# GpSimd waits for its scatters, and at every third indirect store for all stores before it

## The chip, the cores and the metric

One core of a Trainium2 chip runs the kernel. Its engines are TensorE (PE; PEld is its weight load), VectorE (DVE), ScalarE (ACT), GpSimd (POOL) and SyncE (SP), and its DMA engines are fed by queues. The metric is the time on the device in microseconds, the median of several runs.

## The reference

The input x has 2 batches of 2048 rows with 256 columns. A first block normalises x, makes q, k and v by a two-layer perceptron with GELU each, takes causal scores without a softmax, multiplies them with v, normalises the result and adds it to x. A second block normalises again and applies to every row one of eight 256 by 256 matrices, chosen by the row's position alone:

```python
x = x + attn(layernorm(x), W1q, b1q, W2q, b2q, ..., ln_w, ln_b)
# attn: q, k, v = gelu(x@W1+b1)@W2+b2; scores = (q@k.T)/scale * tril; out = layernorm(scores@v)*ln_w+ln_b
# ffn: idx = argmax(pe @ sign(tile_sigs).T); out[b, s] = x[b, s] @ W[idx[s]].T + b[idx[s]]
x = x + ffn(layernorm(x), tile_sigs, W, b)
```

## The kernel before

**Stages.** The attention runs in 8 steps `s` of 512 rows (4 chunks of 128), four for each batch; `LAST` is 7. Front work of step s+1 (transposes, perceptrons, scores) is woven by hand with back work of step s (state, output, normalisation). Every engine has one instruction stream, in the order in which the code issues it, and waits on semaphores.

**Sorting.** A finished chunk of rows, with its scale, shift and row number, lies in `xres`. GpSimd writes its 128 rows with an indirect DMA into `sorted_rows` in DRAM, at places sorted by matrix (`rows_sorted`, line 1674, the scatter at line 1679; 30 scatters in all, semaphores `row_out[s % 3]`). `rstd_out` and `rstd_x1` are small GpSimd steps that give the scales which the rows need before they can be scattered.

**Slots.** The sorted rows are read back as 37 slots of 128 rows (`SLOTS`), n = 0 to 36, all rows of a slot with one matrix. SP loads them (`load_slot`, line 454). It loads slots from n = 17 (`FIRST`) once the scatters of steps up to 6 have landed, and slots from n = 21 (`EARLY`) once all 30 have. Slot 0 is worked alone, then come 18 pairs: pair m holds slots 2m+1 and 2m+2. For a pair ACT normalises both slots (line 982), PE transposes them (line 761), ACT and DVE split the result in two parts (lines 999 and 1429), PE multiplies with the matrix (line 491), and DVE adds the product to the rows (`pair_out`, line 1437), which raises `y_done`. From pair 8 on PE's order is transposes of pair m+2, then products of pair m. So the products of pair 8 stand behind the transposes of pair 10, whose slots are 21 and 22.

**Outs.** GpSimd stores slot n to the output with an indirect DMA (`slots`, line 1741, the store at line 1744), in the order of n; rows that are padding are dropped by the bounds check. The store of slot n is called out n here. Outs 0 to 3 (`REUSED` is 4) raise `sent[0]`, outs 4 to 36 raise `sent[1]`, by 16 each.

**Order on GpSimd in the last part.** Scatters of step 5, outs 0 to 2, `rstd_out(6)`, outs 3 to 6, `rstd_x1(6)`, four scatters of step 6, outs 7 to 12, `rstd_out(7)` of two chunks, outs 13 and 14, `rstd_x1(7)`, the last two scatters, outs 15 and 16, `rstd_out(7)` of the other two chunks, outs 17 and 18, `rstd_x1(7)`, outs 19 to 36.

**The end.** The last two chunks of rows are not sorted. They are multiplied with all eight matrices (`dense_products`, 8 groups of products) and DVE adds what is theirs (`dense_out`, line 1451); SP stores them (line 479). The program ends when these two stores and all outs have landed (lines 481 to 483).

Of the kernel before, what the change touches and what calls it, by code (L numbers as in the profile page):

```python
# [40 lines left out]
LAST = STEPS - 1  # L41
# [23 lines left out]
XR = 3  # L65
# [7 lines left out]
def mk_seq_kernel(nc, x, w1, w2, bias_cols, rows3, sigs2, ffn_w, ffn_b, pe, out):  # L73
# [5 lines left out]
    with ExitStack() as ctx:  # L79
# [6 lines left out]
        def sem(name):  # L86
            return ctx.enter_context(nc.semaphore(name))
# [137 lines left out]
        row_out = [sem(f"row_out{i}") for i in range(XR)]  # L225
# [70 lines left out]
        REUSED = SLOTS - ALL_ROWS  # L296
        in_hT = sb("slot_rows", [P, T_ROWS, ROW])

        def row_buf(n):
            i = n % ALL_ROWS  # L300
            if i < H_ROWS:
                return in_h32[:, i * ROW:i * ROW + ROW]
            return in_hT[:, i - H_ROWS]
# [71 lines left out]
        sent = [sem(f"sent{i}") for i in range(2)]  # L375
# [29 lines left out]
        def sent_before(s):  # L405

            return [16 * (CH * len(range(i, s, XR)) - (DENSE if s > LAST and i == LAST % XR else 0))
                    for i in range(XR)]
# [1198 lines left out]
        def _(pool):  # L1607
# [41 lines left out]
            def rstd_out(s, cs=range(CH)):  # L1649
                part, these = s + 1, slice(cs[0], cs[-1] + 1)  # L1650
                if s < LAST:
                    pool.wait_ge(o_sq, CH * s + CH)
                    nc.gpsimd.tensor_scalar(ve2[:, :], sq2[:, :], 1.0 / C, EPS, ALU.mult, ALU.add).then_inc(var2, 1)
                else:
                    part = s + 1 + cs[0] // 2
                    pool.wait_ge(o_aggr, cs[-1] + 1)
                    nc.gpsimd.tensor_tensor(ve2[:, these], mv2[:, these, 1], eps[:, these], ALU.add).then_inc(var2, 1)
                pool.wait_ge(var2, part)
                nc.gpsimd.tensor_tensor(rs2[:, these], ve2[:, these], half[:, these], ALU.pow).then_inc(rstd2, 1)

            def rstd_x1(s, cs=range(CH)):
                part, these = s + 1 + (s == LAST) * (cs[0] // 2), slice(cs[0], cs[-1] + 1)
                if s < LAST:
                    pool.wait_ge(aggr3, part)
                    nc.gpsimd.tensor_scalar(nm3[:, :], mv3[:, :, 0], -1.0, None, ALU.mult)
                    nc.gpsimd.tensor_tensor(ve3[:, :], mv3[:, :, 1], eps[:, :], ALU.add).then_inc(var3, 1)
                pool.wait_ge(var3, part)
                nc.gpsimd.tensor_tensor(xres[s % XR][:, these, RSTD], ve3[:, these], half[:, these], ALU.pow
                                        ).then_inc(rstd3, 1)
                pool.wait_ge(rstd3, part)  # L1670
                nc.gpsimd.tensor_tensor(xres[s % XR][:, these, SHIFT], nm3[:, these], xres[s % XR][:, these, RSTD],
                                        ALU.mult).then_inc(shift3, 1)

            def rows_sorted(s, cs):

                pool.wait_ge(shift3, s + 1 + (s == LAST) * (cs[0] // 2))
                for c in cs:
                    at = slot_i[:, s // PER, CH * (s % PER) + c:CH * (s % PER) + c + 1]
                    pool.indirect_dma_start(out=sorted_rows, out_offset=bass.IndirectOffsetOnAxis(ap=at, axis=0),  # L1679
                                            in_=xres[s % XR][:, c, :], in_offset=None).then_inc(row_out[s % XR], 16)  # L1680
# [60 lines left out]
            def slots(ns):  # L1741
                for n in ns:
                    pool.wait_ge(y_done, n + 1 if n < AMID else AMID + (n - AMID) // 2 + 1)
                    pool.indirect_dma_start(out=out_rows,  # L1744
                                            out_offset=bass.IndirectOffsetOnAxis(
                                                ap=row_buf(n)[:, PLACE:PLACE + 1].bitcast(I32), axis=0),
                                            in_=row_buf(n)[:, 0:C], in_offset=None,
                                            bounds_check=NB * T - 1, oob_is_err=False).then_inc(sent[n >= REUSED], 16)
# [21 lines left out]
            s = LAST - 1  # L1770
            residual(LAST)
            rstd_x1(s - 1)
            rows_sorted(s - 1, range(CH))
            slots((0, 1, 2))
            rstd_out(s)
            slots((3, 4, 5, 6))
            rstd_x1(s)
            rows_sorted(s, range(CH))

            slots((7, 8, 9, 10, 11, 12))  # L1780
            rstd_out(LAST, (0, 1))
            slots((13, 14))
# [60 lines left out]
```

## Time and profile before

| | us |
|---|---|
| three runs | 315.4, 316.1, 316.92 (median 316.1) |
| the profiled execution | 315.08 |
| its span | 313.3 |
| busy: PE, DVE, ACT, POOL | 289.5, 235.7, 188.7, 176.6 |
| 37 outs on POOL (line 1744), busy | 21.7 + 15.5 |
| 30 scatters on POOL (line 1679), busy | 31.3 |

The span runs from the first instruction to the last; 1.8 us of the execution lie around it. POOL is busy for 56% of the span and PE for 92%, but these are means over the whole. The last 70 us, in which the outs run, are what matters here. The busy time of a scatter or an out on POOL is the writing of its descriptors; its data move after that.

### The profile page before, as it was taken

To read this page: it belongs to the slowest core of one execution; us is meant where nothing else is said; L and a number is where in the kernel's file an instruction comes from. 1 tells how busy PE (TensorE), PEld (TensorE's weight loads), DVE (VectorE), ACT (ScalarE), POOL (GpSimd) and SP (SyncE) were. 2 spreads that over 40 slices of the span, in tenths; PEclk is the share of its full clock that TensorE was granted. 3 is DMA by queue.
4 is the path that set the end of the run, shared out by engine and by line. 5 is a ranking of instruction groups with operands and counts; after the bars stand their busy time and mean duration, and the time that the engine had idled before them with its cause. 6 is when DMAs were issued, how large, how long until landed. Compare 5 with 4: busy or idle time off the path is not lost.

```text
span 313.3 us, 5485 instructions
## 1 busy us (share of the span) xinstructions
PE 289.5 (92%) x1806; PEld 256.9 (82%) x1806; DVE 235.7 (75%) x539; ACT 188.7 (60%) x380; POOL 176.6 (56%) x238
## 2 busy tenths in 40 slices
PE   8999999998999999999999999999998976594994
PEld 6788898986898988889788988899988965583983
DVE  5868788899879879968986896798568667272556
ACT  2646777666756876676778667678664353372400
POOL 6881633351584659475646626584565757276551
PEclk9979999999999999999999999999999999699899
DMA  7909960020011110311221000250142331832011
GB/s 221 231 0 330 354 216 1 0 69 33 6 68 67 42 64 2 94 43 39 63 73 64 9 0 20 85 167 20 70 132 78 114 131 69 256 133 80 32 42 34
DMA packets 24209, 27.83 MB, mean 89 GB/s; under 512 B 4659, under 2 KB 22068, under 8 KB 24118
## 3 DMA queue, kind: packets, MB, share of 16 engines
q1 hardware_dynamic: 15910, 13.68, 14.8%
q0 software_dynamic: 3296, 8.64, 8.0%
q10 hardware_dynamic: 4976, 5.16, 4.9%
q8 instruction: 15, 0.25, 0.3%
q14 instruction: 12, 0.10, 0.1%
HBM read 13.95 MB, written 14.44 MB: 91 GB/s over the span
## 4 chain that ended last, share of the span: by engine, by line
PE 73%; DVE 11%; issue 5%; ACT 4%; another core or an unknown queue 2%; POOL 2%; DMA 1%; DVEq 0%; ACTq 0%; POOLq 0%; SPq 0%
PE ring L491 41%; PE o_ps L491 9%; PE s_ps L491 6%; PE w_ps L491 2%; ACT xn L982 2%; DVE xres L1451 2%; PE ring L500 2%; PE ring L519 2%; PE sc_ps L604 2%; PE ring L761 1%; POOL out_dram L1744 1%; PE sc_ps L602 1%; DVE xres L1219 1%; DVE xnT L1147 1%
## 5 line engine op out<-in xcount | busy, mean ns | idle before, releaser
L491 PE MATMUL ring<-xnT,w_sp 128*128 128x512 f32 x288 | 74.4, 403 | 3.0 <-DVE hT L1152 1.1
L491 PEld LDWEIGHTS ring<-xnT,w_sp 128*128 128x128 f32 x288 | 52.7, 191 | 15.2 <-issue 3.3
L882 ACT ACTIVATE ring<-ring,b_cols 128x512 f32<-128x512 f32 x48 | 31.7, 660 | 28.4 <-PE ring L491 27.0
L491 PE MATMUL ring<-hT,w_sp 128*128 128x512 f32 x192 | 46.8, 398 | 0.0
L1152 DVE TENSOR_TENSOR hT<-ring,hT 128x512 fp32r<-128x512 f32 x48 | 32.5, 681 | 14.6 <-ACT hT L885 13.0
L491 PEld LDWEIGHTS ring<-hT,w_sp 128*128 128x128 f32 x192 | 35.8, 190 | 8.3 <-DVE hT L1152 0.2
L1679 POOL DMA_INDIRECT sorted_rows<-xres,slot_i x30 | 31.3, 1044 | 8.5 <-issue 6.5
L1645 POOL TENSOR_TENSOR vtok<-v,vtok 128x512 fp32r<-128x512 f32 x14 | 18.0, 1287 | 26.5 <-ACT vtok L902 26.5
L1744 POOL DMA_INDIRECT out_dram<-slot_rows x22 | 21.7, 987 | 18.4 <-DVE slot_rows L1437 13.1
L885 ACT CAST hT<-ring 128x512 fp32r<-128x512 f32 x48 | 28.2, 587 | 1.5
L1219 DVE SCALAR_TENSOR_TENSOR xres<-cen,rs,xres 128x256 f32<-128x256 f32 x32 | 23.7, 754 | 3.2 <-issue 3.2
L491 PE MATMUL s_ps<-vtok,ktok 128*128 128x256 f32 x168 | 24.9, 284 | 0.0
L491 PEld LDWEIGHTS ring<-w_sp,hT 128*128 128x128 f32 x192 | 23.4, 188 | 0.6
L491 PE MATMUL ring<-w_sp,hT 128*128 128x256 f32 x192 | 23.9, 280 | 0.0
L1624 POOL TENSOR_SCALAR nm<-mv 128x4 f32<-128x4 f32 x7 | 1.6, 229 | 39.2 <-DVE mv L1141 39.2
L491 PE MATMUL o_ps<-state,q_eye 128*128 128x256 f32 x116 | 23.3, 293 | 0.0
L491 PEld LDWEIGHTS s_ps<-vtok,ktok 128*128 128x128 f32 x168 | 22.0, 191 | 0.0
L1638 POOL TENSOR_TENSOR xres<-xt,row_stage 128x1024 f32<-128x1024 f32 x8 | 22.0, 2751 | 0.0
L1744 POOL DMA_INDIRECT out_dram<-h x15 | 15.5, 1030 | 10.6 <-DVE h L1437 7.0
L491 PE MATMUL w_ps<-wf,xb 128*128 (+1 forms) x126 | 19.8, 307 | 1.3 <-DVE xb L1429 1.3
L491 PEld LDWEIGHTS w_ps<-wf,xb 128*128 128x128 f32 x126 | 17.9, 201 | 2.7 <-issue 1.8
L1191 DVE TENSOR_TENSOR state<-s_ps,state 128x512 fp32r<-128x512 f32 x27 | 18.3, 679 | 2.1 <-ACT state L918 1.8
(245 smaller groups left out, 680.8 us busy)
## 6 DMA issues: line engine op xcount, KB each, us to landing
sorted_rows<-blank ACTq DMA_DIRECT2D x1, 5032.0 KB, 20.8
xt<-x SPq DMA_DIRECT2D x7, 512.0 KB, 3.5
slot_rows<-sorted_rows SPq DMA_DIRECT2D x22, 136.0 KB
w_stage<-tile_w SPq DMA_DIRECT2D x8, 256.0 KB, 2.7
h<-sorted_rows SPq DMA_DIRECT2D x15, 136.0 KB
xt<-x SPq DMA_DIRECT2D x2, 256.0 KB, 3.0
hT<-position_table POOLq DMA_DIRECT2D x1, 512.0 KB, 9.2
sorted_rows<-xres,slot_i POOLq DMA_INDIRECT x30
```

What stands on the lines that cost most here:

```text
L491: last = te.matmul(o, lhs[k][a], rhs[k][c], start=start and k == 0 and i == 0, stop=stop and k == n - 1 and i == 2, skip_group_check=check)
L500: te.matmul(ring[2][:, :], warm_r[:, 0:P], warm_r[:, :], start=True, stop=True)
L519: last = te.transpose(ring[k][:, cols(c)], xn[:, c, cols(k)], ident[:, :])
L882: nc.scalar.activation(full, ring[(2 + m) % 3][:, :], ACT.Gelu, bias=b1c[:, m // 2, m % 2:m % 2 + 1]).then_inc(gelu, 1)
L885: nc.scalar.copy(hT[:, m, 0, :], full).then_inc(h_hi, 1)
L1152: nc.vector.tensor_tensor(hT[:, m, 1, :], ring[(2 + m) % 3][:, :], hT[:, m, 0, :].bitcast(F32), ALU.subtract).then_inc(h_lo_dve, 1)
L1191: nc.vector.tensor_tensor(state[:, 1, :], s_ps[:, :], state[:, 0, :].bitcast(F32), ALU.subtract).then_inc(s_lo, 1)
L1219: nc.vector.scalar_tensor_tensor(out=xres[s % XR][:, c, 0:C], in0=cen[:, c, :], scalar=rs2[:, c:c + 1], in1=xres[s % XR][:, c, 0:C], op0=A ...
L1638: nc.gpsimd.tensor_tensor(xres[s % XR][:, :, 0:C], xt[s % 2][:, :, :], lnb_row[:, :].unsqueeze(1).broadcast_to([P, CH, C]), ALU.add).then_ ...
L1645: nc.gpsimd.tensor_tensor(vtok[:, 1, 2 * j:2 * j + 2, :], v32[:, 2 * j:2 * j + 2, :], vtok[:, 0, 2 * j:2 * j + 2, :].bitcast(F32), ALU.sub ...
L1679: pool.indirect_dma_start(out=sorted_rows, out_offset=bass.IndirectOffsetOnAxis(ap=at, axis=0), in_=xres[s % XR][:, c, :], in_offset=None) ...
L1744: pool.indirect_dma_start(out=out_rows, out_offset=bass.IndirectOffsetOnAxis(ap=row_buf(n)[:, PLACE:PLACE + 1].bitcast(I32), axis=0), in_= ...
```

## The change

Three waits are added, all on GpSimd. Ahead of out n, for n above 4 and divisible by 3 (n = 6, 9, 12, ..., 36: eleven of them), it waits until `sent[1]` shows that outs 4 to n-1 have all landed. After `rstd_out(6)`, ahead of out 3, it waits until the scatters of step 5 have landed. After the four scatters of step 6, ahead of out 7, it waits until these have landed.

```diff
             def slots(ns):
                 for n in ns:
                     pool.wait_ge(y_done, n + 1 if n < AMID else AMID + (n - AMID) // 2 + 1)
+                    if n > REUSED and n % 3 == 0:
+                        pool.wait_ge(sent[1], 16 * (n - REUSED))
                     pool.indirect_dma_start(out=out_rows,
...
             slots((0, 1, 2))
             rstd_out(s)
+            pool.wait_ge(row_out[(s - 1) % XR], sent_before(s)[(s - 1) % XR])
             slots((3, 4, 5, 6))
             rstd_x1(s)
             rows_sorted(s, range(CH))
+            pool.wait_ge(row_out[s % XR], sent_before(LAST)[s % XR])
 
             slots((7, 8, 9, 10, 11, 12))
```

## Rows read from the trace of the kernel before

**Rows 1.** The page, part 4: the chain that ended last, shares by engine.
```profile
PE 73%; DVE 11%; issue 5%; ACT 4%; another core or an unknown queue 2%; POOL 2%; DMA 1%; DVEq 0%; ACTq 0%; POOLq 0%; SPq 0%
```
**Rows 2.** The same chain in order of time: start us, length us, what.
```profile
248.27 1.76 another core or an unknown queue
...
254.64 0.98 POOL out_dram L1744
...
263.74 2.43 DMA sorted_rows<-xres,slot_i
266.23 2.14 DMA slot_rows<-sorted_rows
...
282.66 4.64 another core or an unknown queue
```
**Rows 3.** Timeline of POOL, 229 to 249: start, length, instruction, [idle before <-releaser].
```profile
229.85 1.07 POOL L1744 DMA_INDIRECT out_dram<-h  x1 [0.20 <-issue]
...
245.32 0.96 POOL L1679 DMA_INDIRECT sorted_rows<-xres,slot_i  x1 [0.30 <-issue]
246.59 1.43 POOL L1744 DMA_INDIRECT out_dram<-h  x1 [0.31 <-issue]
248.32 1.00 POOL L1744 DMA_INDIRECT out_dram<-h  x1 [0.30 <-issue]
```
**Rows 4.** Timeline of POOL, 254 to 262.
```profile
254.64 0.98 POOL L1744 DMA_INDIRECT out_dram<-slot_rows  x1 [2.74 <-DVE slot_rows L1437]
255.93 0.98 POOL L1744 DMA_INDIRECT out_dram<-slot_rows  x1 [0.30 <-issue]
...
258.30 1.04 POOL L1744 DMA_INDIRECT out_dram<-slot_rows  x1 [0.36 <-issue]
259.64 0.98 POOL L1744 DMA_INDIRECT out_dram<-slot_rows  x1 [0.30 <-issue]
261.11 0.72 POOL L1668 TENSOR_TENSOR xres<-ve,half 128x2 f32<-128x2 f32 x1 [0.48 <-issue]
```
**Rows 5.** Timeline of POOL, 274 to 306.
```profile
274.75 1.04 POOL L1744 DMA_INDIRECT out_dram<-slot_rows  x1 [6.43 <-DVE slot_rows L1437]
276.10 0.99 POOL L1744 DMA_INDIRECT out_dram<-slot_rows  x1 [0.30 <-issue]
...
278.65 1.04 POOL L1744 DMA_INDIRECT out_dram<-slot_rows  x1 [0.54 <-DVE slot_rows L1437]
...
305.81 0.97 POOL L1744 DMA_INDIRECT out_dram<-h  x1 [0.30 <-issue]
```
**Rows 6.** Timeline of DVE, 253 to 301.
```profile
253.15 0.69 DVE L1437 TENSOR_TENSOR slot_rows<-w_ps,slot_rows 128x512 f32<-128x512 f32 x1
...
258.69 0.87 DVE L1219 SCALAR_TENSOR_TENSOR xres<-cen,rs,xres 128x256 f32<-128x256 f32 x2
...
260.86 0.16 DVE L1242 TENSOR_SCALAR ve<-mv 128x2 f32<-128x2 f32 x1
...
300.49 0.69 DVE L1437 TENSOR_TENSOR h<-s_ps,h 128x512 f32<-128x512 f32 x1 [3.10 <-remote]
```
**Rows 7.** Timeline of ACT, 268 to 288.
```profile
268.39 1.09 ACT L982 ACTIVATE xn<-slot_rows 128x255 f32<-128x255 f32 x2 [4.12 <-DMA slot_rows<-sorted_rows]
...
287.33 0.58 ACT L999 CAST xb<-sc_ps 128x512 fp32r<-128x512 f32 x1 [4.67 <-remote]
```
**Rows 8.** DMA busy tenths in 40 slices of 0.075 us: from 258.2, then from 305.8.
```profile
DMA  0000000000000000000000496993000000000000
...
DMA  0000110000000000000001159999510000000000
```
**Rows 9.** Timeline of SP's queue, then the landing time of its two output stores.
```profile
306.70 4.84 SPq L479 DMA_DIRECT2D out_dram<-xres  x2
...
DMA to landing us min/median/max: 1.7/1.7/1.7
```
**Rows 10.** The instructions that write `out_dram`: duration ns min/median/max, first and last start.
```profile
L1744 POOL DMA_INDIRECT out_dram<-slot_rows x22: 972/976/1042, 254.6 to 298.1; - x22
```

## The prediction

> **What bounds the kernel now.** I read the chain that ended last first. By shares it is PE for 73% of the span and POOL for 2% [rows 1], so a reader could stop there and call waits on POOL free. The same chain in order of time says more: up to about 248 us it is PE's own stream, and after that it goes through every engine in turn. It passes an out on POOL at 254.64, the last scatter at 263.74 (landed 2.43 us after its start), the load of a slot that needed that scatter (2.14 us), and only then ACT [rows 2]. ACT had been idle for 4.12 us when it got that slot at 268.39 [rows 7]. So POOL's order between 245 and 264 us decides when the last 16 slots can start. I then read POOL's timeline over the last 75 us, because all added waits stand there, and at last DVE's, ACT's and the DMA view to see how long a store takes to land.
>
> Two further things are seen. The chain has pieces that belong to no instruction, 1.76 us at 248.27 and 4.64 us at 282.66 [rows 2]; ACT's and DVE's timelines show them as waits on PE's semaphores that nobody is named for, 4.67 us before ACT at 287.33 and 3.10 us before DVE at 300.49 [rows 6, 7]. And at the very end DVE's dense work and SP's store of it are last: SP's second store ends its issue at 311.54 (306.70 + 4.84) and starts some 0.34 us before, it lands 1.7 us after, at 312.9, and the span ends 0.4 us later [rows 9]. The last out starts at 305.81 [rows 5], so POOL's stream has about 5 us of slack at the end.
>
> **The price of one wait.** Outs that follow each other start 1.28 us apart: 255.93 less 254.64 [rows 4], a busy time of 0.976 us [rows 10] and 0.30 us between. A wait for the out just before it takes the place of that distance by the landing time plus the restart. *Landing:* for the out that starts at 258.30 the DMA engines are busy until slice 28, which is 258.2 + 28 x 0.075 = 260.3, 2.0 us after its start; for the last out (305.81) POOL's few packets are seen in slices 21 to 23, up to 307.6, 1.8 us after [rows 8]. These are ends of data, without the semaphore, so they bound it from below. The scatter with its semaphore took 2.43 us [rows 2], which I take as the upper end without contention. I take 2.3 us for a full slot and 2.1 us for the late, mostly empty ones. *Restart:* no wait of POOL for an out exists in this trace. The nearest rows are outs that waited for DVE: line 1437 on DVE ended at 253.84 (253.15 + 0.69) [rows 6] and the out started at 254.64 [rows 4], 0.80 us later. A tensor instruction after a short wait restarts faster, so 0.3 us (the plain distance between two outs) is the lower end and 0.8 us my value. So an out that waits starts 3.1 us after the one before it and not 1.28 us, a price of 1.82 us (late ones 2.9 us, a price of 1.6 us); the ends are 2.1 and 3.3 us.
>
> The Trainium skill, page DMA: Bandwidth & Descriptors, section Anatomy of one DMA, gives about 2.0 us plus bytes over 436 GB/s for a DMA from GpSimd, 2.3 us for 128 KB. No row here shows its split into parts; with it for all outs the end would come some 0.8 us later than below. The same page, Rules for kernel authors, says to issue early and wait late so that the fixed time is overlapped, which speaks against the change.
>
> **Waits that cost nothing.** The wait ahead of out 3 is for scatters of step 5, which POOL started between 217 and 222 us; with 2.43 us each they are down by 225, and out 3 starts at 229.85 [rows 3]. The wait of out 6 for out 5 delays out 6 by at most 1.82 us, from 235.1 to 237.0. What is behind it, the small steps of `rstd_x1(6)`, waits for DVE until 239.2 anyway; if DVE were 1 us earlier this cover would still hold. The wait of out 15 is for out 14, 5 us and two scatters earlier: nothing.
>
> **Waits on the path to the last scatter.** Here I follow the start times.
> 1. The last scatter of step 6 starts at 245.32 [rows 3]; landed at 247.75 (2.43), restart 0.8: out 7 starts at 248.55 and not at 246.59. Out 8: 249.83.
> 2. Out 9 waits for out 8: 252.93. Out 10: 254.21. Out 11: 255.49, and not 254.64. Its own wait for DVE (2.74 us long) [rows 4] hid the first 3.5 of 4.4 us.
> 3. Out 12 waits for out 11: 258.59, and not 255.93 [rows 4]. This is the dear one, for behind it in POOL's order stands `rstd_out` of the last step, whose result DVE needs at once (line 1219 at 258.69) [rows 6].
> 4. Out 13 follows out 12 by the 2.37 us of before (255.93 to 258.30, with the two small steps between), so 260.96; out 14 at 262.30, over at 263.28. DVE starts line 1219 at about 260.65 and is through with line 1242 2.33 us later (258.69 to 261.02) [rows 6], at 263.0, so out 14 is what ends last. The step at line 1668 starts at 263.30 and not 261.11 [rows 4]: the last two scatters come 2.2 us late.
> 5. SP's load of slot 21 waits for them, ACT gets it at 268.39 + 2.2 = 270.6, and PE's transposes of pair 10 and the products of pair 8 behind them move by the same 2.2 us. No other engine has work to fill that gap: it was already idle there.
>
> **The run of outs at the end.** Out 17 waits for pair 8: 274.75 + 2.2 = 276.94 [rows 5]. Out 18 waits for out 17: 280.04. Out 19 is 2.55 us behind out 18, as before (276.10 to 278.65), 282.59; out 20 at 283.9. From there six outs wait (21, 24, ... 36). I take 3.0 us for each, the mean of full and late ones, and 2 x 1.28 for the two between: out 21 at 286.9, and out 36 five rounds of 5.56 us later at 314.7. DVE does not hold them any more: before, the outs of pair 16 waited for line 1437 at 300.49 [rows 6], and out 33 would now start at 309. Out 36 lands 2.1 us after its start, 316.8, and with the 0.4 us of before the span ends at 317.2.
>
> The dense end moves with step 5 only: 313.3 + 2.2 = 315.5 if all else stays. So POOL takes over as the bound, with 1.7 us over the dense end. The span grows by 317.2 - 313.3 = 3.9 us. The profiled execution was 315.08 us, 1.0 us under the median of the three runs, so I add the difference to both alike: 319.0 for an execution like the profiled one, and 320.0 us against the median of 316.1.
>
> **The rivals.**
> *A, dense end last.* If landing and restart together are near their lower end (2.5 us and less), POOL is done before the dense end. Then only the shift of the last scatters counts, 2.2 us or, with cheaper waits, down to 1.0 us: 317.1 to 318.3, say 318.0. For it: both terms are bounds from other instructions. Against: 0.80 us and 2.43 us are direct rows.
>
> *B, the other side: PE's late semaphores go away.* The waits on PE that nobody is named for lie where POOL has issued four or more indirect DMAs without a pause: from 241.4 to 251.9, from 278.65 to 288.6 and from 291.8 to 299.1, and none lies before 217 us, where POOL issues at most two in a row. If the run of DMAs is what holds PE's semaphores up, a pause after every third ends it. The 4.64 us at 282.66 are on the chain [rows 2], and of the 3.10 us at 300.49 [rows 6] some 0.8 us, since PE's dense products bound DVE after that. With the scatters' shift cut to 0.8 us (waits at 2.4 us) the dense end would come at 313.3 + 0.8 - 3.1 - 0.8 = 310.2 (I count 3.1 of the 4.64 us, as the work behind it catches its own pace). It decides only if POOL's outs end before that, and this needs each wait to cost under about 2.4 us from start to start: then 316.8 - 9 x 0.7 = 310.5. This gives 310.5 + 0.4 or so, 3 us faster: 313.2 us. If the stalls go but a wait costs 3.1 us, nothing is won, since POOL is last by then: the stalls are no longer on the path. For B: the places agree. Against: no row links them, and the price of a wait would have to be far below the rows.
>
> *C, the waits do not bite.* If landing is mostly done when the wait is reached, nothing changes: 316.1. Against: the out waited for is always the one just before, 1.28 us earlier, and its data are moving later than that [rows 8].
>
> *D, landing stretched.* Slot loads run at 249 to 254 and 268 to 277 us beside outs 8, 17 and 18. If a landing there takes 3.5 us, and the late ones 2.43 us, the end is 2 to 3 us later: 322.5.
>
> **How the numbers follow.** Forecast 320.0 with chance 0.70, A 0.11, B 0.06, C 0.04, D 0.09. A measurement of this kernel tells 0.5% (1.6 us) from no change. The forecast's own width: each of nine waits may be off by 0.2 us, so 318.2 to 321.8. The range takes in A and most of D: 317.4 to 322.6. Slower by over 0.5% (above 317.7): forecast, D and most of A, 0.87. Same: C, the rest of A, 0.07. Faster: B, 0.06.
>
> **What would show it.** In the profile after, out 9, 12, 18, 21 and each third one start about 3 us after the one before, the others 1.28 us. The step at line 1668 is near 263.3, ACT's first slot of the last 16 near 270.6, the last out near 314.7, and the chain ends in outs on POOL and not in DVE's line 1451. If the waits without a name at 282 and 300 are gone and the dense work ends near 310, half of B is right although the time is slower. Wrong would be: a distance of 2.4 us or less, or out 12 not ahead of DVE's line 1219.

## The result: 3.5% slower, three times the forecast loss

| | before | changed |
|---|---|---|
| median of 4 runs, us | 316.2 | 327.5 |
| lowest and highest, us | 315.4, 316.9 | 326.5, 328.4 |
| profiled execution, us (its span) | 315.1 (313.3) | 326.9 (325.2) |

The ratio is 1.035, with a 95% interval of 1.032 to 1.039. The forecast was 320.0 us with a range to 322.6: the sign was right, and the time lies outside the range.

The chain that ended last, in order of time (start, length, what), now runs through outs on GpSimd. This is its last part:

```profile
294.40 0.70 DVE slot_rows L1437
295.14 0.52 issue
296.24 0.90 issue
297.15 0.98 POOL out_dram L1746
298.43 2.14 DMA out_dram<-slot_rows
...
314.13 0.98 POOL out_dram L1746
315.41 2.07 DMA out_dram<-h
317.60 0.51 issue
318.10 1.20 POOLq L79
```

Each round is the landing of an out, two pieces of issue, and one out beside the next. That is the forecast picture, and the answer to [rows 2]. The first line is misleading. It names DVE because DVE's line 1437 ended at 295.1, just before out 24 started, but that was the work of pair 15. DVE had finished out 24's own pair, pair 11, at 285.1. What out 24 waited for was out 23, started at 292.61 (3.26 us earlier, as in the other rounds). So the path runs on through GpSimd's outs, back to outs 17 and 18. The last line is not in the forecast: a piece of GpSimd's queue at line 79, after which the span still goes on to 325.2.

The timeline of POOL shows the waits (start, length, instruction, [idle before <-who ended it]):

```profile
245.58 0.96 POOL L1679 DMA_INDIRECT sorted_rows<-xres,slot_i  x1 [0.31 <-issue]
249.99 1.00 POOL L1746 DMA_INDIRECT out_dram<-h  x1 [3.46 <-DMA sorted_rows<-xres,slot_i]
...
257.32 0.99 POOL L1746 DMA_INDIRECT out_dram<-slot_rows  x1 [0.30 <-issue]
260.60 0.98 POOL L1746 DMA_INDIRECT out_dram<-slot_rows  x1 [2.29 <-DMA out_dram<-slot_rows]
...
265.40 0.75 POOL L1668 TENSOR_TENSOR xres<-ve,half 128x2 f32<-128x2 f32 x1
266.23 0.20 POOL L1671 TENSOR_TENSOR xres<-nm,xres 128x2 f32<-128x2 f32 x1
266.72 1.04 POOL L1679 DMA_INDIRECT sorted_rows<-xres,slot_i  x1 [0.29 <-POOL xres L1671]
268.06 0.96 POOL L1679 DMA_INDIRECT sorted_rows<-xres,slot_i  x1 [0.30 <-issue]
...
315.41 0.97 POOL L1746 DMA_INDIRECT out_dram<-h  x1 [0.30 <-issue]
318.33 0.97 POOL L1746 DMA_INDIRECT out_dram<-h  x1 [1.94 <-DMA out_dram<-h]
```

Out 12 starts 3.28 us behind out 11, the last out 2.92 us behind the one before it. The last scatter starts at 268.06, where it was 263.74 [rows 2], and the last out at 318.33, where it was 305.81 [rows 5]. ACT and DVE answer [rows 6, 7]:

```profile
272.70 1.15 ACT L982 ACTIVATE xn<-slot_rows 128x255 f32<-128x255 f32 x2 [10.48 <-DMA slot_rows<-sorted_rows]
...
287.59 0.59 ACT L999 CAST xb<-sc_ps 128x512 fp32r<-128x512 f32 x1 [0.75 <-PE sc_ps L761]
...
308.63 1.07 DVE L1451 SCALAR_TENSOR_TENSOR xres<-o_ps,w_stage,xres 128x256 f32<-128x256 f32 x2 [0.33 <-PE o_ps L491]
```

ACT's line 999 waits 0.75 us and no longer 4.67, and DVE's dense work ends at 309.70. Before, it ended at 311.2:

```profile
310.11 1.07 DVE L1451 SCALAR_TENSOR_TENSOR xres<-o_ps,w_stage,xres 128x256 f32<-128x256 f32 x2
```

So the late waits are gone, and the dense end came earlier although its start moved 4.3 us later.

What comes after the last out is seen with the instructions of line 79, the end of the program (count, duration ns, first and last start). Before:

```profile
L79 POOLq DRAIN  x1: 9007/9007/9007, 303.4 to 303.4; - x1
```

Changed:

```profile
L79 POOLq DRAIN  x1: 6830/6830/6830, 318.1 to 318.1; - x1
L79 SPq COMPARE_BRANCH  x1: 38/38/38, 320.5 to 320.5; - x1
...
L79 SPq EVENT_SEMAPHORE  x1: 17/17/17, 325.1 to 325.1; - x1
```

GpSimd's drain ended at 312.4 before (303.4 + 9.0) and at 324.9 now. Both are 6.6 us after the start of the last out, and 5.6 us after its 0.97 us of issue. SP had all landings by 320.5 and then had to wait for it. So GpSimd's stream did not have 5 us of slack at the end: it had about 0.5 us (312.4 against the dense landing at 312.9). The last out moved by 12.5 us (305.81 to 318.33) and the span grew by 11.9. The sentence ahead of the prediction that the program ends when all stores have landed leaves this drain out.

The granted clock was lower, 0.954 over the span against 0.977. It isn't what cost the time: PE's wait for the late scatters lies in there, and the way from ACT's first late slot to out 17 took 6.42 us (272.70 to 279.12) where it had taken 6.36 (268.39 to 274.75).

### The profile page after: what moved, and what is told of

Same layout as the page of the kernel before. It is cut to its first block, busy times and chain, and to the rows that moved or that the text cites. A ratio compares the mean times of both kernels' runs of the same rounds, so it can differ in the third digit from the quotient of the medians.

```text
span 325.2 us, 5498 instructions
## 1 busy us (share of the span) xinstructions
PE 287.7 (88%) x1806; PEld 254.8 (78%) x1806; DVE 235.9 (73%) x539; ACT 188.9 (58%) x380; POOL 176.5 (54%) x238
## 4 chain that ended last, share of the span: by engine, by line
PE 68%; DVE 10%; issue 7%; DMA 5%; ACT 4%; POOL 4%; POOLq 1%; SPq 0%; ACTq 0%; DVEq 0%
PE ring L491 39%; PE o_ps L491 9%; PE s_ps L491 5%; POOL out_dram L1746 3%; DMA out_dram<-slot_rows 3%; ACT xn L982 2%; PE ring L500 2%; PE w_ps L491 2%; PE ring L519 1%; PE sc_ps L604 1%; PE ring L761 1%; PE sc_ps L602 1%; DVE xres L1219 1%; DVE xnT L1147 1%; PE sc_ps L761 1%
## 5 line engine op out<-in xcount | busy, mean ns | idle before, releaser
L1746 POOL DMA_INDIRECT out_dram<-h x15 | 14.8, 990 | 20.1 <-DMA out_dram<-h 7.9
L491 PE MATMUL w_ps<-wf,xb 128*128 (+1 forms) x126 | 18.8, 295 | 1.0 <-DVE xb L1429 1.0
L491 PEld LDWEIGHTS o_ps<-state,q_eye 128*128 128x128 f32 x116 | 18.5, 189 | 1.3 <-issue 0.3
```

What stands on the lines that cost most here:

```text
L491: last = te.matmul(o, lhs[k][a], rhs[k][c], start=start and k == 0 and i == 0, stop=stop and k == n - 1 and i == 2, skip_group_check=check)
L1746: pool.indirect_dma_start(out=out_rows, out_offset=bass.IndirectOffsetOnAxis(ap=row_buf(n)[:, PLACE:PLACE + 1].bitcast(I32), axis=0), in_= ...
```

## The experiments

Each ratio is against the kernel before on the same chip, with its 95% interval.

### Only the waits for scatters

```diff
+            pool.wait_ge(row_out[(s - 1) % XR], sent_before(s)[(s - 1) % XR])
             slots((3, 4, 5, 6))
...
             rows_sorted(s, range(CH))
+            pool.wait_ge(row_out[s % XR], sent_before(LAST)[s % XR])
```

> Only the two waits for scatters, none at the outs. Theory (a wait costs only where it moves the last two scatters or the last out): out 7 starts near 249.7 us of the span, the outs behind it 1.28 us apart catch up with DVE's work by out 11, the last scatters move by 0.4 us at most, and the time is that of the kernel before within 0.6 us (316.2). Rival (the wait for the scatters alone is a large part of the loss, since it came out 1.4 us dearer than forecast): 318 or more.

Ratio 1.0012 (0.9986 to 1.0038). Out 7 started at 249.29, 4.26 us after the last scatter of its group (245.03), and the last scatter at 264.18. Outs 8 to 11 ran 1.3 to 1.5 us apart, and out 11 was at 254.65, where it had stood before. The wait is dearer than forecast, but it is covered, since out 11 had waited for DVE before. Alone it costs nothing that can be measured.

### Only the waits at outs 6 to 18

```diff
+                    if n in (6, 9, 12, 15, 18):
+                        pool.wait_ge(sent[1], 16 * (n - REUSED))
```

> Only the waits at outs 6, 9, 12, 15 and 18; outs 19 to 36 run without a pause. Theory: the last two scatters move by about 2.3 us (outs 9 and 12), and since outs 19 and on run without a pause, ACT's unexplained wait on PE near 285 us of the span (4.7 us in the kernel before) is there again; the time is 318.0 to 319.0. Rival (that wait has nothing to do with pauses in GpSimd's DMAs and merely did not happen after the shift): the wait stays away and the time is 314 to 316.5.

Ratio 1.015 (1.011 to 1.019), 320.3 us. The last scatter came 24.4 us after the first scatter of the group before it started (240.70 to 265.07). Before, that was 22.4 us (241.36 to 263.74): a shift of 2.0 us, near the expected 2.3. But the late wait did not only come back, it was twice as long. ACT's timeline:

```profile
287.08 1.09 ACT L982 ACTIVATE xn<-h 128x255 f32<-128x255 f32 x2
297.99 0.58 ACT L999 CAST xnT<-ring 128x512 fp32r<-128x512 f32 x1 [9.81 <-remote]
```

PE stood idle for 9.29 us there, and in the 6 us from 300 on it had a granted clock of 0.59. Both fit a loss above the expected 2 to 3 us; how much each cost wasn't measured. This execution (321.7) was also the slowest of four, so the 9.81 us need not be typical. The rival, that the wait had merely not happened, fell.

### Only the waits from out 21 on

```diff
+                    if n >= 21 and n % 3 == 0:
+                        pool.wait_ge(sent[1], 16 * (n - REUSED))
```

> Only the waits at outs 21, 24, ... 36. The scatters stay where they were. Theory (the program ends about 5.6 us after GpSimd's last DMA instruction, by its drain): out 36 starts near 311.6 us, the drain ends near 318.2 us, the time is 321 (5 us slower), and ACT's unexplained wait at 283 to 287 us is gone. Rival (the end is set by the landing of the last out, as the forecast had it): out 36 lands at 313.9, the span ends at 314.3 and the time is 317.2.

Ratio 1.017 (1.014 to 1.019), 320.7 us. The last out started at 312.24, and the instructions of line 79 say:

```profile
L79 POOLq DRAIN  x1: 6830/6830/6830, 312.0 to 312.0; - x1
L79 SPq COMPARE_BRANCH  x1: 38/38/38, 314.4 to 314.4; - x1
...
L79 SPq EVENT_SEMAPHORE  x1: 17/17/17, 319.0 to 319.0; - x1
```

All had landed by 314.4, and the span ended 4.7 us later with the drain. ACT and DVE had no wait without a name after 260 us, and DVE's dense work ended at 305.4 and not at 311.2. So the same pauses brought the dense end 5.8 us forward and GpSimd's end 6.4 us back.

### Only the last three outs wait

```diff
+                    if n in (34, 35, 36):
+                        pool.wait_ge(sent[1], 16 * (n - REUSED))
```

> Only waits at outs 34, 35 and 36, each for all outs before it; nothing else depends on these outs. Theory (drain): out 36 starts 3 x 1.7 us later, near 310.9 us of the span, the drain ends 6.6 us after that start at 317.5, and the time is 320.5 (4.3 us slower). Rival (landing): out 36 lands at 313.0, just at the dense end, and the time is 316.2 to 316.8. ACT's unexplained wait at 283 to 287 us stays in both, as the outs before 34 run without a pause.

Ratio 1.010 (1.007 to 1.013), 318.2 us. Nothing depends on these outs but the end of the program. The last out started at 309.37, the drain ended 6.6 us later at 316.0, and SP had all landings at 312.7. The landing rival is refuted. The loss is smaller than expected, mainly because out 33 started at 299.46 in this run and not at 302.0.

### The changed kernel without its wait at out 12

```diff
-                    if n > REUSED and n % 3 == 0:
+                    if n > REUSED and n % 3 == 0 and n != 12:
```

> The changed kernel without its wait at out 12, all other waits as they are. Theory (out 12 stands ahead of the steps that the last two scatters need, and everything behind is in one chain on GpSimd): out 12 starts 1.28 us behind out 11 and not 3.28, the last scatter and the last out move 2.0 us earlier, and the time is 2.0 us under that of the changed kernel (8.5 to 9.5 us over the kernel before). Rival (DVE's or PE's work sets the last scatters by then): under 0.5 us is won.

Ratio 1.032 (1.027 to 1.036), where the changed kernel had 1.035; the two intervals overlap, so the medians alone don't settle it. The traces do: the last scatter started at 266.32 and not 268.06, the last out at 316.43 and not 318.33, and the span was 323.3 and not 325.2. One wait, 1.9 us.

### Two waits only, at outs 22 and 26

```diff
+                    if n in (22, 26):
+                        pool.wait_ge(sent[1], 16 * (n - REUSED))
```

> Only two waits, at outs 22 and 26, for all outs before them. Theory (PE's unexplained late semaphores come after four or more indirect DMAs in a row; GpSimd's drain sets the end 6.6 us after the last out starts): outs 19 to 21, 22 to 25 are short runs, so ACT's wait near 285 us is gone; the last out starts near 304.3 us and the drain ends at 310.9, 2 us before the end of the kernel before; a late wait may come back after 295 us, in the run of outs 26 to 36, and cost a part. Time 0.3 to 2.2 us under the kernel before. Rival (each wait costs its 1.9 us at the end, as in the run with waits from out 21 on): 1 to 3 us over it.

Ratio 0.9954 (0.9936 to 0.9972): faster than before. The last out started at 304.17 (304.3 expected). From 291.37 on eleven outs ran without a pause, and the late waits came back, in the dense work. DVE's timeline:

```profile
307.02 1.07 DVE L1451 SCALAR_TENSOR_TENSOR xres<-ring,w_stage,xres 128x256 f32<-128x256 f32 x2 [3.17 <-remote]
```

### A pause by other work, without a wait for a landing

```diff
+                    if n >= 21 and n % 3 == 0:
+                        if n > 21:
+                            pool.wait_ge(idle_s, n // 3 - 7)
+                        nc.gpsimd.tensor_tensor(idle_t[:, :, :], row_stage[:, 0:2, :], row_stage[:, 0:2, :],
+                                                ALU.add).then_inc(idle_s, 1)
```

> No wait for a landing; in place of the waits at outs 21, 24, ... 36 GpSimd adds two 512-column tiles (about 1.3 us, result unused, a side product that leaves the output alone). Theory a (any pause in the run of DMA instructions on GpSimd ends PE's late semaphores): the waits without a name between 280 and 301 us are gone, DVE's dense work ends near 305.5, the last out starts near 308.3 and the drain ends at 314.9: 1 to 2.5 us slower than the kernel before. Theory b (it is the landing that must be waited for): the wait of 4 to 5 us near 285 us stays, DVE's dense work ends at 311 or later.

Ratio 0.9984 (0.9964 to 1.0004). POOL's timeline of one round:

```profile
285.59 1.07 POOL L1749 TENSOR_TENSOR idle_t<-row_stage 128x512 f32<-128x512 f32 x1
286.82 0.99 POOL L1751 DMA_INDIRECT out_dram<-slot_rows  x1 [0.17 <-POOL idle_t L1749]
288.12 0.97 POOL L1751 DMA_INDIRECT out_dram<-slot_rows  x1 [0.30 <-issue]
289.40 0.97 POOL L1751 DMA_INDIRECT out_dram<-slot_rows  x1 [0.31 <-issue]
```

Three outs take 4.79 us. No wait without a name was left after 260 us, and the dense work ended at 305.4. So no landing has to be waited for: theory b fell. The last out started at 305.98 and not at the expected 308.3, so the run wasn't the 1 to 2.5 us slower that I had expected. The drain ended at 312.6 and took the gain back.

### One more wait at the very end

```diff
             slots(range(19, SLOTS))
+            pool.wait_ge(sent[1], 16 * (SLOTS - REUSED))
```

> The kernel before, with one more wait at the very end of GpSimd's stream: for the landing of all outs. The last out starts near 305.8 us and lands at 307.9. If the drain's 6.6 us count from the last out's start, it ends at 312.4 as before and the time is the same within 0.2 us; if the drain needs its 5.6 us after the wait, it ends at 313.5 and the span is 0.3 us longer; if the drain waits for landings, it becomes short and ends soon after 308, and the span stays at 313.3 by the dense store.

One execution only: 314.2 us, beside a median of 314.6 before. The last out started at 302.86, earlier than before (the late waits fell a little differently here, and outs 33 and on were early). The wait was over by 305.4, and:

```profile
L79 POOLq DRAIN  x1: 5623/5623/5623, 305.4 to 305.4; - x1
```

With nothing left to land, the drain still took 5.62 us, from the end of the wait. So it isn't a wait for landings. In the other thirteen traces it ended 6.6 to 6.7 us after the start of the last out, 5.6 to 5.7 after its issue. What GpSimd does in it no row shows.

### Pauses that are too short

```diff
+                    if n >= 21 and n % 3 == 0:
+                        nc.gpsimd.memset(idle_t[:, n:n + 1], 0.0)
```

> As the run with two-tile additions, but the instruction put between the DMAs at outs 21, 24, ... 36 is a store of zeros to one column of scratch (about 0.1 us busy). Theory (it is enough that the run of indirect DMA instructions on GpSimd is broken by another instruction): the waits without a name after 260 us are gone, DVE's dense work ends near 305.4 and lands near 307.5, the last out starts near 301.5 and the drain ends near 308.3; the span is 308 to 309.5 and the time 4 to 6 us under the kernel before. Rival (the pause must have a length of 1 us or more): the 4 to 5 us wait near 285 us is there, and the time is within 1 us of the kernel before.

Ratio 0.9984 (0.9966 to 1.0001). Here the theory as I had put it fell. ACT's timeline has the wait as before:

```profile
286.64 0.59 ACT L1000 CAST xb<-sc_ps 128x512 fp32r<-128x512 f32 x1 [4.31 <-remote]
```

The reason is in POOL's timeline: outs 21 and 24 are at 280.65 and 284.49, 3.84 us for three, no more than without the store (3 x 1.28). The store fits into the gap between two DMA instructions. It breaks the run, but gives no free time.

> The same, with such an instruction also ahead of outs 0, 7 and 9, where runs of 4 scatters and 1 to 4 outs stand. Theory: ACT's waits without a name at 222 to 224 and at 248 to 253 us are shorter or gone as well; the first is not on the chain, the second moves the last scatters earlier by up to 1 us; the time is 0 to 1 us under the run without them. Rival (no gain from them, each costs about 0.3 us on GpSimd): the same or 0.5 us more.

With more such stores, ahead of outs 0, 7 and 9 (`if n in (0, 7, 9) or n >= 21 and n % 3 == 0`): ratio 0.9991 (0.9973 to 1.0008), and waits of 2.06, 2.24 and 4.29 us. Nothing changed.

For 256 columns in place of 512 in the added tiles:

> The additions at outs 21, 24, ... 36 with 256 columns and not 512, so that three outs take about 4.3 us; it was 4.8 with 512 columns (no late waits) and 3.84 with the one-column store (all late waits). Theory (free time between the DMA instructions is what counts, and half is enough): the 4 us wait near 285 us is gone, the last out starts near 303.3, the drain ends near 309.9, and the time is 2.5 to 4 us under the kernel before. Rival (0.5 us in three outs is too little): the wait is there at 2 us or more and the time is within 1.5 us of the kernel before.

Ratio 0.9963 (0.9936 to 0.9989). Three outs took 4.37 us. The wait near 285 was gone, but two came later in ACT's timeline, so that neither theory was right as put, and the gain, 0.4% or 1.2 us, was under half of the expected one (2.5 to 4 us). The profiled execution was the slowest of twelve (317.4 us against a median of 315.7), so its late waits need not be those of most:

```profile
291.89 0.59 ACT L1001 CAST xnT<-ring 128x512 fp32r<-128x512 f32 x1 [2.91 <-remote]
...
297.05 0.59 ACT L1001 CAST xb<-sc_ps 128x512 fp32r<-128x512 f32 x1 [3.59 <-remote]
```

### The 512-column pause where it is needed only

```diff
-                    if n >= 21 and n % 3 == 0:
+                    if n in (21, 24, 27, 30):
```

> The additions with 512 columns at outs 21, 24, 27 and 30 only; outs 30 to 36 run without a pause. Theory (late semaphores need a long run; GpSimd's last out plus 6.6 us is the end otherwise): no wait without a name between 280 and 298 us, a late one of up to 3 us in DVE's dense work after 300 us, the last out starts near 304.1, the drain ends near 310.7, and the time is 1 to 2.5 us under the kernel before and under that of the run with all six additions. Rival (the dense work, held up after out 30, is then last): the span is 312.5 or more.

The diff is against the run with six such additions. Ratio 0.9914 (0.9884 to 0.9944), 313.8 us: the lowest ratio of all, 4.2% under the changed kernel by the two ratios. Its interval just touches that of the run with two waits. The gain on this chip, 3.0 us by the medians, is above the expected 1 to 2.5. No wait without a name was left after 260 us, but the lateness was not gone. In the dense work behind the last pause PE's last products ended at 306.13 by their record, and DVE started on them at 307.55, 1.4 us later (0.03 us in the run with six additions):

```profile
304.57 1.56 PE L493 MATMUL o_ps<-wf,xb 128*128 128x512 f32 x6
...
307.55 1.07 DVE L1453 SCALAR_TENSOR_TENSOR xres<-o_ps,w_stage,xres 128x256 f32<-128x256 f32 x2 [1.11 <-PE o_ps L493]
```

That was covered, as GpSimd was last again. The last out started at 305.18 and the drain ended at 311.8 (296.8 + 15.0), 0.2 us before the end of the span:

```profile
L79 POOLq DRAIN  x1: 15005/15005/15005, 296.8 to 296.8; - x1
...
L79 SPq COMPARE_BRANCH  x1: 38/38/38, 310.4 to 310.4; - x1
```

## Why the prediction was wrong

The span ended at 325.2 and not at 317.2. The 8.0 us divide by the forecast's own steps.

| step | forecast | measured | error, in all |
|---|---|---|---|
| out 7, after the wait for scatters | 248.55 | 249.99 | 1.4 |
| out 12 | 258.59 | 260.60 | 2.0 |
| line 1668, ahead of the last scatters | 263.30 | 265.40 | 2.1 |
| out 18, behind out 17 | 3.1 | 3.76 | 2.8 |
| out 36 | 314.7 | 318.33 | 3.6 |
| from the start of out 36 to the end | 2.5 | 6.9 | 8.0 |

**The step that failed** is the last one, and behind it the sentence that POOL's stream has about 5 us of slack at the end. I took the landing of the last out as GpSimd's end. It is 5.6 us of drain after the issue, and this ended at 312.4 before, almost level with the dense end. The drain cost 4.4 of the 8.0 us (6.9 in place of 2.5). It shows in no busy row, since it is an instruction of the queue; the instructions of line 79 in the trace of before have it. The runs with waits from out 21 on and at the last three outs show it: their landings were complete 4.7 and 3.5 us before their spans ended.

**The right mechanism at a wrong size** is the other 3.6 us. The restart of 0.80 us held: in the last round the landing ended at 317.48 (315.41 + 2.07) and the out started at 318.33, 0.85 later. The landing was 2.07 to 2.43 us where neither slot loads nor code moved, as forecast, and the six late waits cost 2.92 to 3.26 us from start to start (3.0 forecast). The Trainium skill (DMA: Bandwidth & Descriptors, Anatomy of one DMA) gives about 2.0 us and the bytes over 436 GB/s, which is an estimate of 2.3 us for 128 KB; these landings agree with it. But the waits beside other traffic were far off: from the last scatter to out 7 4.4 us in place of 3.2, from out 17 to out 18 3.76 in place of 3.1, from out 5 to out 6 4.52 (233.98 to 238.50). Slot loads moved beside outs 5 and 17. Beside the scatter the DMA view has a packet of the kind "instruction", that is, code. Such a packet also stands beside the two dear waits of other runs where no slot was loaded: 3.67 us (286.15 to 289.82, waits from out 21 on) and 3.71 us (302.72 to 306.43, last three outs). In none of the changed kernel's six late waits (2.92 to 3.26 us) is there one. So the places agree, but no run took the packets away. My rival D named such stretched landings with 9%, and priced them at 2.5 us. One number of the working was wrong without harm: out 11's own wait for DVE hid 2.4 of 3.3 us by the start times that stand there, not 3.5 of 4.4, and both leave the same 0.9.

**The covers.** Out 3 and out 15 cost nothing, as forecast. The cover of out 6 nearly held, though out 6 came at 238.50 and not by 237.0: the small steps behind it started at 239.50, where they had been at 239.26. Out 12 as the dear wait held: without it the last scatter came 1.7 us and the end 1.9 us earlier.

**Rival B** had its first half right: with pauses, PE's late semaphores are gone, and the dense end comes 5.8 us earlier (the run with waits from out 21 on). I had counted 3.9 us. Its point of decision, 2.4 us from start to start, left the drain out, so with these waits it could not decide. It does with a cheaper pause: 4.79 us for three outs and only four of them gave the lowest ratio. Rivals A and C fell: a wait cost 2.9 to 4.5 us from start to start, and the dense end was not last.

**What stays open** is how GpSimd's DMAs hold up what comes from PE. The profile models the ends of PE's matmuls, so it can't tell whether the semaphore was late or the product itself. The runs show the dose:

| three outs take, us | late waits of ACT or DVE between 280 and 301 us |
|---|---|
| 3.84 (no pause; one-column store) | 1.6 to 4.7 us before, up to 9.8 in other runs, from the fourth or fifth out on |
| 4.37 (256 columns) | 1.7 to 3.6 us, later (one slow execution) |
| 4.79 (512 columns) | none |
| 5.7 (waits, mean) | none |

That fits a backlog which grows when DMAs come faster than one in about 1.5 us (an estimate: 4.37 / 3 is late, 4.79 / 3 is not), but no row shows the backlog.

## What to carry to other kernels

Read each engine's last instruction, with its drain, and not the landing of its last DMA, before calling its stream slack. A wait for the DMA just issued costs landing plus restart each time, here 1.6 to 3.2 us over the 1.28 us without it, and it hurts most where small steps that others wait for stand behind it in the queue. If the aim is to space DMAs out, spacing them by other work, and only as long as someone is hurt by the run, gave the same effect here for half of the price (0.95 us for each pause, 4.79 less 3.84, and not about 1.85).

## What the runs showed of the hardware that was not expected

- GpSimd's drain at the end of the program took 5.6 to 5.7 us in every trace after its last instruction or wait, also with all its DMAs landed (5.62 us).
- While GpSimd issued indirect DMAs of 128 rows every 1.28 us, ACT or DVE started 2 to 9 us after the end of the TensorE record that they waited for (2.0 us at 284.50 before; 9.1 us at 297.99 with waits at outs 6 to 18). With three DMAs in 4.79 us they started on time.
- The time from the start of an indirect store to the restart of a waiting GpSimd was 2.9 to 3.3 us with neither slot loads nor code beside it, 4.5 us beside slot loads, and 3.7 us in the two late rounds with a code packet and no slot load.
